# Folded attention's output kept on chip: values stationary in column quarters, projection over row quarters, ring fetched by SyncE

## The reference, cut to what matters

```
        qkv = x @ Wqkv.T + bqkv
        qkv = qkv.reshape(B, H, S, 3 * hd)
        q, k, v = jnp.split(qkv, 3, axis=-1)
        scores = jnp.einsum('bhsd,bhtd->bhst', q, k) * (1.0 / math.sqrt(hd))
        attn = jax.nn.softmax(scores, axis=-1)
        vals = jnp.einsum('bhst,bhtd->bhsd', attn, v)
        vals = vals.reshape(B, S, D)
        return vals @ Wo.T + bo
```

## Time and profile before

| what | value |
|---|---|
| median of the timed runs | 1656.15 us |
| the profiled execution's own time | 1649.57 us |
| its span in the trace | 1647.8 us |
| PE busy | 1446.8 us (88%) |
| DVE busy | 926.8 us (56%) |
| ACT busy | 762.1 us (46%) |
| DMA moved | 181.19 MB, mean 110 GB/s |
| one PE record of 32 columns on 128 moving columns | 274 ns (group of L1852) |
| one PE record of 32 columns on 256 moving columns | 379 ns (median, L1558) |

### The profile page before, as it was taken

The page is one execution under the profiler, slowest core; times in us unless marked ns, Lnnn a source line. Parts: engine busy times, 40 slices in busy tenths (PEclk is TensorE's granted clock), DMA queues, the critical chain, the costliest instruction groups (busy, mean ns, idle before and its releaser), DMA issues. The chain is left out here.

```text
span 1647.8 us, 29080 instructions
## 1 busy us (share of the span) xinstructions
PE 1446.8 (88%) x11204; PEld 1088.0 (66%) x11204; DVE 926.8 (56%) x2764; ACT 762.1 (46%) x1782; POOL 91.8 (6%) x86
## 2 busy tenths in 40 slices
PE   7999989976499858899999999999997876768996
PEld 6978979853277643467777777777775872546765
DVE  5654455554676312377777777777775453453434
ACT  6744535423122200266666666666665941212222
POOL 2300000000000200200000000000000000000000
PEclk9999999977799979999999999999999996899999
DMA  9945424111232479600100001001000302206860
GB/s 336 336 151 203 146 81 144 67 39 66 83 134 90 156 278 367 233 35 35 35 35 35 35 35 35 35 35 35 2 1 2 125 1 118 108 0 211 278 252 4
DMA packets 63464, 181.19 MB, mean 110 GB/s; under 512 B 7264, under 2 KB 43232, under 8 KB 62048
## 3 DMA queue, kind: packets, MB, share of 16 engines
q1 hardware_dynamic: 59488, 160.18, 26.8%
q0 software_dynamic: 3264, 12.58, 1.9%
q10 hardware_dynamic: 576, 6.58, 1.0%
HBM read 178.68 MB, written 0.66 MB: 109 GB/s over the span
## 5 line engine op out<-in xcount | busy, mean ns | idle before, releaser
L1916 ACT ACTIVATE cross_s<-cross_s,cross_shift 128x896 f32<-128x896 f32 x224 | 215.1, 1031 | 38.7 <-DVE cross_shift L2000 38.7
L1910 ACT COPY cross_eT<-cross_ring 128x512 f32<-128x512 f32 x280 | 153.1, 591 | 143.4 <-PE cross_ring L1838 143.4
L1838 PEld LDWEIGHTS cross_ring<-consts,cross_s 128*128 128x128 f32 x1568 | 168.2, 141 | 56.3 <-issue 44.2
L1838 PE MATMUL cross_ring<-consts,cross_s 128*128 128x128 f32 x1568 | 197.0, 277 | 6.1 <-ACT cross_s L1916 6.1
L1991 DVE CUSTOM_DVE_ANT_0 cross_s<-cross_scores,cross_mask,cross_top 128x448 f32<-128x448 f32 x224 | 141.3, 681 | 84.8 <-PE cross_scores L1830 84.7
L436 ACT ACTIVATE slots_probs<-slots_scores,slots_bias,ctx_rinv 128x128 f32<-128x128 f32 x294 | 130.1, 462 | 108.1 <-DVE slots_bias L484 108.1
L1991 DVE CUSTOM_DVE_ANT_0 cross_s<-cross_scores,cross_mask,cross_half_max 128x448 f32<-128x448 f32 x224 | 141.4, 680 | 13.3 <-PE cross_scores L1830 13.3
L155 PE MATMUL slots_scores<-slots_qkT,slots_ctxT 128*128 128x128 f32 x1176 | 138.3, 275 | 7.9 <-DMA slots_ctxT<-in_ctxT 7.1
L155 PEld LDWEIGHTS slots_scores<-slots_qkT,slots_ctxT 128*128 128x128 f32 x1176 | 136.8, 192 | 11.9 <-DMA slots_ctxT<-in_ctxT 8.1
L386 PE MATMUL slots_attended<-ctx_rows,slots_probs 128*128 128x257 f32 x588 | 135.2, 380 | 1.2 <-DVE slots_pooled L498 1.1
L1830 PE MATMUL cross_scores<-cross_keysT,cross_qz 32*128 32x448 f32 x896 | 121.8, 588 | 3.9 <-DVE cross_half_max L1991 2.7
(11 more groups left out here) (774 smaller groups left out, 2116.0 us busy)
## 6 DMA issues: line engine op xcount, KB each, us to landing
slots_ctxT<-in_ctxT SPq DMA_DIRECT2D x42, 896.0 KB, 4.6
ctx_rows<-in_ctx_rows SPq DMA_DIRECT2D x28, 896.0 KB, 7.8
ring_w<-in_moe_w POOLq DMA_DIRECT2D x12, 1024.0 KB, 16.4
ring_w<-in_moe_w SPq DMA_DIRECT2D x12, 1024.0 KB, 10.5
cross_ctxT<-in_ctxT SPq DMA_DIRECT2D x13, 896.0 KB, 4.5
padded_ctxT<-in_ctxT SPq DMA_DIRECT2D x12, 896.0 KB, 4.5
plain_ctxT<-in_ctxT SPq DMA_DIRECT2D x12, 896.0 KB, 4.6
local_layers<-in_w_local SPq DMA_DIRECT2D x2, 4806.0 KB, 14.3
```

What stands on the lines that cost most here:

```text
L1838: last = pe.transpose(bank(("turn", u, t))[:, j * P:(j + 1) * P], s_buf[:, u % 2, j, t * P:(t + 1) * P], K.ident)
L1910: act.copy(eT[:, u % 2, t], bank(item)).then_inc(st("emptied_act"), 1)
L1916: act.activation(rows, rows, ACT.Exp, bias=shift[:, u % 2, j:j + 1], scale=SCALE).then_inc(st("exp"), 1)
```

## The change

1. **The output stays on chip.** `fold_o`, its write and its read, the turning of `o2` and the 18 idle products ahead of it are gone. ACT's exponentials also sum their rows (`accum_out`), DVE takes the reciprocals and multiplies the probabilities before they are turned. The values are now the stationary operand, 32 columns wide (16 channels and 16 zeros), and the turned probabilities the moving one. Group g writes its four heads to column quarter g, so `oT_mm` holds channel by position, 32 partitions for each quarter and 512 columns.
2. **The projection** takes its input from there. Channel block b of a quarter is every sixteenth column of `oT`, 32 of them, which are 32 rows of the output. 16 blocks by 4 quarters are 64 products, each of 32 rows (16 of them zeros) by 32 columns, on 256 moving columns; quarter g reads row quarter g and writes partitions of quarter g of `y_mm`. Its weights lie for that as 128x4096 (`fold_out`, 2.1 MB instead of 0.26 MB), and are fetched by ACT behind `fold` at the start of the padded stage.
3. **The copies of the turned probabilities** are shared: ACT makes three, DVE the last. DVE adds `bo` ahead of the first product.
4. **The ring's couples 0 to 2** are fetched by SP behind its read of `folded`. POOL does nothing in the stage.

```
 FOLD_OUT_SPEC = [("wo", FOLDS * D)]       # FOLDS = D // HEAD16, FOLD_QUARTER = 32
 # sync
-                sp.wait_ge(st("o"), 1)
-                sp.dma_start(o_heads, o[:, :].rearrange("p (h d) -> p h d", d=HEAD16)).then_inc(st("o_out"), 16)
-                sp.wait_ge(st("o_out"), 16)
-                sp.dma_start(o2[:, :], T["fold_o"]).then_inc(st("o2_in"), 16)
+                sp.wait_ge(st("folded_in"), 16)
+                for p in range(SLOTS - 1):
+                    K.ring.fetch_w1(sp, p)
+                    K.ring.fetch_w2(sp, p)
 # scalar
-                exponentials_scalar(act, st, "sdpa", pr, heads, small[:, 0, :], HEADS16, 4)
+                def exponentials(g):
+                    act.wait_ge(st("sdpa_top"), g + 1)
+                    for hd in range(4 * g, 4 * g + 4):
+                        last = act.activation(pr[:, hd], heads[:, hd], ACT.Exp, bias=small[:, 0, hd:hd + 1], accum_out=small[:, 1, hd:hd + 1])
+                    last.then_inc(st("sdpa_exp"), 1)
+
+                def copy(g):
+                    act.wait_ge(st("sdpa_probsT_mm"), g + 1)
+                    act.copy(prT[:, 4 * g:4 * g + 4], headsT[:, 4 * g:4 * g + 4]).then_inc(st("sdpa_probsT"), 1)
+
+                exponentials(0)
+                exponentials(1)
+                for g in range(2, 4):
+                    exponentials(g)
+                    copy(g - 2)
+                copy(2)
                 root_table(act, K)
-
-            @block.gpsimd
-            def _(pool):
-                pool.wait_ge(st("folded_in"), 16)
-                for p in range(SLOTS - 1):
-                    K.ring.fetch_w1(pool, p)
-                    K.ring.fetch_w2(pool, p)
 # tensor
-                attend16(pe, K, st, "sdpa", heads, headsT, pr, prT, v, o_mm)
-                idle_products(pe, K, mm, 18)
-                pe.wait_ge(st("o2_in"), 16)
-                transposes(pe, oT_mm, o2, K.ident, DC).then_inc(st("oT_mm"), 1)
+                def turn(g):
+                    pe.wait_ge(st("sdpa_probs"), g + 1)
+                    for hd in range(4 * g, 4 * g + 4):
+                        last = pe.transpose(headsT[:, hd], pr[:, hd], K.ident)
+                    last.then_inc(st("sdpa_probsT_mm"), 1)
+
+                def attend(g):
+                    pe.wait_ge(st("sdpa_probsT"), g + 1)
+                    quarter = slice(FOLD_QUARTER * g, FOLD_QUARTER * (g + 1))
+                    for i in range(4):
+                        last = pe.matmul(oT_mm[quarter, i * P:(i + 1) * P], v[:, 4 * g + i], prT[:, 4 * g + i], start=True, stop=True)
+                    return last
+
+                for g in range(4):
+                    turn(g)
+                    if g:
+                        attend(g - 1)
+                K.weights.wait(pe, "fold_out")
+                attend(3).then_inc(st("oT_mm"), 1)
                 pe.wait_ge(st("oT"), 1)
-                product(pe, y_mm, [(oT[:, c], wo[:, c]) for c in range(DC)]).then_inc(st("y_mm"), 1)
+                for b in range(FOLDS):
+                    for g in range(4):
+                        quarter = slice(FOLD_QUARTER * g, FOLD_QUARTER * (g + 1))
+                        last = pe.matmul(y_mm[quarter], of_fold[quarter, :, b], wo[quarter, b], start=b == 0, stop=b == FOLDS - 1)
+                last.then_inc(st("y_mm"), 1)
 # vector
-                copies_vector(dve, st, "sdpa", prT, headsT, 4)
-                outputs16(dve, link, st, o, o_mm, small[:, 1, :])
+                link(dve.tensor_tensor(K.x, K.x, W["bo"], ALU.add))
+                for g in range(4):
+                    some = slice(4 * g, 4 * g + 4)
+                    dve.wait_ge(st("sdpa_exp"), g + 1)
+                    link(dve.reciprocal(small[:, 2, some], small[:, 1, some]))
+                    dve.tensor_tensor(pr[:, some], pr[:, some], spread(small[:, 2, some], P), ALU.mult).then_inc(st("sdpa_probs"), 1)
+                dve.wait_ge(st("sdpa_probsT_mm"), 4)
+                dve.wait_ge(st("sdpa_probsT"), 3)
+                dve.tensor_copy(prT[:, 12:16], headsT[:, 12:16]).then_inc(st("sdpa_probsT"), 1)
                 dve.wait_ge(st("oT_mm"), 1)
                 dve.tensor_copy(oT[:, :], oT_mm).then_inc(st("oT"), 1)
-                link(dve.tensor_tensor(K.x, K.x, W["bo"], ALU.add))
                 residual_vector(dve, st, K.x, y_mm, "y_mm")
```

More of the change, by code:

```diff
@@ L1205, in _ @@
                 K.weights.fetch(act, "fold")
+                K.weights.fetch(act, "fold_out")
                 flash.scalar(act)
@@ L1279, in _ @@
                 residual_vector(dve, st, K.x, flash.acc[:, 0:D], "pooled")
-FOLD_SPEC = [("wqkv", DC * 3 * D), ("bqkv", 3 * D), ("wo", DC * D), ("bo", D), ("head_mask", 8)]
+FOLD_SPEC = [("wqkv", DC * 3 * D), ("bqkv", 3 * D), ("bo", D), ("head_mask", 8)]
+FOLDS = D // HEAD16
+FOLD_OUT_SPEC = [("wo", FOLDS * D)]
+FOLD_QUARTER = 32
 def stage_folded_attention(nc, K, T):
@@ L1291, in stage_folded_attention @@
         W = K.weights.parts("fold")
-        wqkv, wo = chunks(W["wqkv"], 3 * D), chunks(W["wo"], D)
+        wqkv, wo = chunks(W["wqkv"], 3 * D), chunks(K.weights.parts("fold_out")["wo"], D)
         h = st.sb("h", [P, D])
@@ L1297, in stage_folded_attention @@
         q = st.sb("q", [P, 2, D])
-        v = st.sb("v", [P, HEADS16, HEAD16 + 1])
+        v = st.sb("v", [P, HEADS16, FOLD_QUARTER])
         qT = st.sb("qT", [P, DC, P])
@@ L1302, in stage_folded_attention @@
         prT = kblk[:, :].rearrange("p c h k -> p (c h) k")
-        o = st.sb("o", [P, D])
-        o2 = st.sb("o2", [P, D])
-        oT = st.sb("oT", [P, DC, P])
-        small = st.sb("small", [P, 2, 16])
+        oT = st.sb("oT", [P, 4 * P])
+        small = st.sb("small", [P, 3, 16])
         lnb = norm_buffers(st, "ln")
@@ L1312, in stage_folded_attention @@
         T_mm = mm[:, 1024:1536].rearrange("p (a c k) -> p a c k", a=2, k=P)
-        o_mm = sc[:, 0:HEADS16 * (HEAD16 + 1)].rearrange("p (h d) -> p h d", d=HEAD16 + 1)
-        oT_mm = sc[:, 512:512 + D].rearrange("p (c k) -> p c k", k=P)
+        oT_mm = sc[:, 0:512]
+        of_fold = oT[:, :].rearrange("p (m b) -> p m b", b=FOLDS)
         y_mm = sc[:, 1024:1024 + D]
         qkv_heads = T["fold_qkv"].rearrange("t c -> (t c)").rearrange("(h s c) -> s h c", h=HEADS16, s=P)
-        o_heads = T["fold_o"].rearrange("t c -> (t c)").rearrange("(h s c) -> s h c", h=HEADS16, s=P)
         with nc.Block() as block:
@@ L1386, in _ @@
                 dve.tensor_tensor(qkv[:, :], mm[:, 0:3 * D], W["bqkv"], ALU.add).then_inc(st("qkv"), 1)
-                dve.memset(v[:, :, HEAD16:], 1.0).then_inc(st("v"), 1)
+                dve.memset(v[:, :, HEAD16:], 0.0).then_inc(st("v"), 1)
                 dve.wait_ge(st("folded_in"), 16)
@@ L2832 @@
     "quant_up": (UP_SPEC, width(SLOT_SPEC) + width(GATE_SPEC) + width(PATT)), "quant": (QUANT_SPEC, 0), "padded": (PADDED_SPEC, width(QUANT_SPEC) + DC * QFFN),
+    "fold_out": (FOLD_OUT_SPEC, width(QUANT_SPEC) + DC * QFFN + width(PADDED_SPEC) + 2 * DC * GROUP),
     "fold": (FOLD_SPEC, 0), "moe": (MOE_SPEC, width(FOLD_SPEC)), "cross": (CROSS_SPEC, width(FOLD_SPEC) + width(MOE_SPEC)),
-    "delta": (DELTA_SPEC, width(FOLD_SPEC) + width(MOE_SPEC) + width(CROSS_SPEC)),
+    "delta": (DELTA_SPEC, max(DIAGONALS * P, width(FOLD_SPEC) + width(MOE_SPEC) + width(CROSS_SPEC))),
     "mqa": (MQA_SPEC, 0), "hashed": (HASH_SPEC, width(MQA_SPEC)),
@@ L2889, in layouts @@
     g = lambda n: a["L1_attn_" + n]
-    out["w_fold"] = packed(FOLD_SPEC, dict(wqkv=in_chunks(g("Wqkv").T), bqkv=on_all(g("bqkv")), wo=in_chunks(g("Wo").T),
+    of_quarter = np.zeros((4, FOLD_QUARTER, FOLDS, D), f)
+    of_quarter[:, 0:HEAD16] = g("Wo").T.reshape(FOLDS, HEAD16, D).transpose(1, 0, 2)
+    out["w_fold_out"] = packed(FOLD_OUT_SPEC, dict(wo=of_quarter.reshape(P, FOLDS * D)))
+    out["w_fold"] = packed(FOLD_SPEC, dict(wqkv=in_chunks(g("Wqkv").T), bqkv=on_all(g("bqkv")),
                                            bo=on_all(g("bo")), head_mask=(i // HEAD16 == np.arange(8)[None, :]).astype(f)))
@@ L2946, in layouts @@
     return out
-SCRATCH = {"fold_qkv": (P, 3 * D), "fold_o": (P, D)}
+SCRATCH = {"fold_qkv": (P, 3 * D)}
 class Kept:
```

## The result

The changed kernel takes **1636.32 us** (median of 4 runs, 1633.06 to 1644.92), the kernel before in the same measurement 1658.25 (1654.65 to 1662.29). The ratio is 0.9877, 95% interval 0.9855 to 0.9899. The profiled execution took 1644.92 us, the longest of its four; its span is 1643.1. Outside the two stages in question it spent 10.7 us more than the trace before (1643.1 - 1647.8 + 15.4; slots 375.5 against 371.4 us, local attention 113.2 against 108.6, and smaller ones), though all that the change does there is one larger fetch in the padded stage.

A forecast was written before the change was run, and what follows sets the result against it. Bound by a DRAM round trip behind POOL's ring transfers, the gain capped by the ring's DMA flow: 15.6 us off the profiled 1649.57 gives 1634.0, and 1640.5 against the median 1656.15; range 1634 to 1651.

The forecast's parts named there:

- keep its distance: After the last wait for weights: the last couples' products and the cross stage follow unchanged, so the gain is 15.6 us.
- What bounds the kernel: Folded stage's end: 24.5 us without useful work, waiting for a 128 KB DRAM trip behind POOL's twelve transfers; DMA caps the gain.
- POOL loses 10 us of issuing that nothing waited for: Folded stage: taking the ring's issuing from POOL was put at no cost and no gain.
- The end of the chain: Folded stage on PE, DVE and ACT, exponentials to `oT` copy: values' products end at 575.9, copy at 576.6 us.
- gaps of about 1 us: New chain before the projection: PE's waits are about 1 us at most, which speaks against a fall of its clock.
- The projection: Folded stage: 128 records at 0.050 us side by side, 6.8 us, ending at 583.5; engines' chain ends at 584.5.
- The 28.4 us: Rival for the projection: quarters run one after another at 0.22 us a record; chance 0.06 at full clock, 0.03 at half.
- SP's queue: Folded stage's end: SP's twelfth ring transfer is let in at 585.5, so experts start at 586, 1.5 us behind the engines.
- rival that SP is held to the last landing: SP gets free only when the twelfth transfer lands at 595.2, experts start at 595.6, time 1649; chance 0.06.
- The cap by DMA: Ring flows without gap from 560.34; couple 7's first weights land at 644.3 instead of 659.93, gain 15.6 us.
- 1.3 us in hand: Experts' stage: couple 4 is asked for at 602.7, and the queue stays full if that comes by 604.0.
- Costed at nothing: Larger projection weights (2.1 MB) fetched in the padded stage, dropped idle products and POOL's lost issuing: no effect on time.

The follow-up runs named there:

- e2: Changed kernel, but POOL instead of SP fetches the ring's couples 0 to 2; ratio to the kernel before 0.9978.
- e4: Changed kernel, projection loops exchanged: all 16 blocks of one quarter before the next quarter; projection 47.3 us instead of 7.2, kernel 1.5% slower than before.
- e8: Changed kernel, but SP issues the ring right behind the qkv read without waiting for it to land; sum of both stages 100.6 us.
- e9: Changed kernel, ring issued without waiting for the qkv read and its first 2 MB asked for at the folded stage's start; sum of both stages 100.9 us.
- e10: Changed kernel, SP fetches two couples ahead instead of three, the third with the fourth at the experts' start; sum of both stages 106.5 against 101.9 us.
- e5: Kernel before without the 16 transfers that refill the ring, couples 4 to 7 using weights of 0 to 3; experts' stage 58.6 us instead of 69.2.
- e6: Changed kernel without the 16 transfers that refill the ring, couples 4 to 7 using weights of 0 to 3; experts' stage 56.9 us instead of 69.2.
- e1: Changed kernel run again unchanged, against the kernel before; ratio 0.9884.
- e12: Changed kernel run once more unchanged, against the kernel before; ratio 0.9910.
- e3: Kernel before, but POOL starts the ring only after the output has come back from DRAM; 0.84% slower.
- e7: Kernel before, with the DRAM trip kept, but SP fetches the ring's couples 0 to 2 ahead of the output's write; ratio 1.0000.

## Why the prediction was right, step by step

The forecast was 1640.5 us; 1636.32 was measured, and 1640.2 is the mean of all runs. The gain was given as 15.6 us, and 15.4, 13.1 and 17.1 were read in the two stages. Both close agreements are partly luck. The forecast started from 1656.15, and the runs of before have a mean of 1658.2, so the timed gain is 18.0 and not 15.6. And the 15.4 of the first trace is made of two misses that cancel: the flow of weights was 1.5 us faster than I had it (82.5 us to the last wait's end instead of 84.0), and what follows it did not "keep its distance" but took 1.6 us longer, at a clock of 0.88.

- **What bounds the kernel.** Right as far as it went: the trip is gone and the stage is 15.5 us shorter. It was incomplete, though. Behind the trip, with POOL still fetching the ring, lay POOL's hold, which would have kept the stage to 0.8 us after 596.2. The step that failed is "POOL loses 10 us of issuing that nothing waited for", a term that the prediction puts at nothing. The issuing cost nothing, but the landing of what POOL had issued did. Had SP not taken over the ring, my sum would have given the same 15.6 us, and e2 shows 6.4 (117.3 - 110.9; 602.75 - 597.0 would be 5.8), and 0.22% in the timed runs (0.01 to 0.43%, so 6.4 us, 0.39%, lies within). What I had costed as a load on SP brought the other 9.0 of the 15.4 us.
- **The end of the chain.** The copy to `oT` came 16.5 us after the first ring issue (581.11 - 564.64), predicted 15.6 (575.9 - 560.34). The values' products of the first group are about half of the difference: 8 records in 1.79 us instead of 0.86. Without that, PE could have begun the next values at 576.33 + 0.61 = 576.9, when ACT's copy was done, and began them at 577.52. The prediction held that gaps of about 1 us speak against a fall of the clock; but PE stood still for 2.15 us ahead of its first turning, and its clock was 0.57 from 573 to 577 and 1.00 from 577 to 582.
- **The projection.** Predicted 6.8 us, measured 7.17. Less the last record's own time, as in the prediction's sum, that is 0.054 a record, where the 1.93 us row gave 0.050. The rule of the Trainium skill ("TensorEngine Tiling (Array Packing)", Gotcha 1: PSUM Pressure), that different row tiles cannot access the same PSUM bank simultaneously, does not agree with this: four row quarters wrote four partition quarters of one bank at the rate of side-by-side products. The 28.4 us that it would have given are excluded. e4 shows what no overlap is like.
- **SP's queue.** Predicted: held, let in at 25.2 after the first issue, 1.5 us behind the engines. Measured: SP free at 591.08, 26.4 after it, and 1.6 us behind the engines (589.51). e8, e9 and e10, in which SP is free earlier, save 1.2 us of stage, so the hold is real and small. What was off is the lead of 9.6 us by which a transfer is let in ahead of its landing: the twelfth landed 35.0 us after the first issue (predicted 34.9) and was let in 8.6 us before that. The rival that SP is held to the last landing is excluded, since the stage ended some 8 us before it.
- **The cap by DMA.** The flow has no gap, and couple 7's first weights release PE 82.5 after the first issue, predicted 84.0. e5 and e6 show that this flow bounds the stage. The margin for couple 4's request was thinner than "1.3 us in hand": e1 asked 43.1 after its first issue, within my limit of 43.7, and the DMA share fell all the same; e8 asked at 43.6 (603.01 - 559.38) and its share stayed at 1.09, but its flow ran later. The 253 GB/s that the prediction names for the stretch 602.7 to 619.4 is that of 602.7 to 607.1; the stretch has 251, and nothing hangs on it.
- **Costed at nothing.** The padded stage, where the 2.1 MB `fold_out` is fetched, takes 107.7 us from its first instruction to the next stage's in both traces. That step holds.
- **What came besides.** The experts' preamble runs at full clock: 15.0 us to couple 4's request instead of 16.7. The forecast left that out of the cap. e5 against e6 shows that it is worth 1.7 us (58.6 - 56.9) where the flow doesn't bound the stage; where it does, it is margin for couple 4's request.

What stays open: the timed means differ by 18.0 us and the two stages by 15.2 on average of three traces. From the spread of the runs the 18.0 has a standard error of 1.6 us, so 15.2 lies within two of them. The intervals of e1 and e12 include 0.9907, which 15.4 us would give; that of the first measurement doesn't. The rest of a trace varies by several us between executions of one program, so it isn't shown that 3 us come from elsewhere, nor that they don't. Nor is it shown by what means POOL holds the stage's end, whether by the engine or by what the program does where a block ends, only that the end follows the landing by 0.8 us twice.

## What to carry to other kernels

When a long wait is removed, ask of every engine that meets at the stage's end what it still has under way, and of an engine that issues transfers when they land, not when it has issued them. A gain can need two edits that each give next to nothing alone (0.2% and 0.0% here, 1.2% together). Where the next stage is bound by a flow of transfers, moving the stage's start pays only as far as the flow's next request can follow: here a flow begun 3 us earlier gave 1.3 us (e8), with 2 MB more ahead of it 0.8 us (e9), and a flow with a hole cost 4.6 us (e10).

## What the runs showed of the hardware

- A barrier of all engines opened 0.8 us after the last transfer issued by POOL had landed, in e2 and in e3, with all engines idle for 10.8 and 28.7 us. SP's transfers don't do that: in the changed kernel the next stage began at 591.52, and SP's last transfer, asked for at 585.57 and let in at 591.08, landed at 599.7.
- Products of 32 rows by 32 columns on 256 moving columns took 0.054 us a record with the four quarters in turn, at a clock of 1.00, and 0.29, then 0.38 within one quarter, at a clock of 0.72 (21 records in 6.15 us) and 0.50 (109 in 41.0).
- A write of 128 KB took 22.4 us to land with POOL's twelve transfers of 1 MB ahead of it, 10.0 us behind SP's own (e7), and 3.0 us with free queues (e3).
- PE's clock before the qkv write was 1.00 in some executions and about 0.8 in others of the same program (1.00 in the changed kernel's first trace, 0.79 in e1, 0.82 in e12), which is worth 1.5 us there.
